# Moving GpSimd's rounding and scaling of the last attention head to other engines, and reordering four hand-overs of a mixture-of-experts layer

## What is computed

```
x = x + attention(layernorm(x))     # 12 heads of 32, scores + row bias + column bias, softmax, @ w_proj + b_proj
t = layernorm(x)                    # 8 groups of 128 tokens
probs = softmax(t @ w_router); gate, idx = top_k(probs, 2)
slot of a token in its expert = running count within the group, first choices ahead of second; at most C = 40
expert_in[e] = dispatch^T @ t       # (8 groups * 40 slots) x 384
out = combine @ (relu(expert_in[e] @ wi[e]) @ wo[e])     # wi 384 x 1536, wo 1536 x 384, 8 experts
x = x + out
```

## Time and profile before

| | |
|---|---|
| median of 3 executions | 580.09 us (579.93 to 580.94) |
| the profiled execution | 579.37 us, its span 577.6 us |
| TensorE, matmuls | busy 561.6 us, 97% |
| VectorE | 389.5 us, 67% |
| ScalarE | 281.2 us, 49% |
| GpSimd | 192.5 us, 33% |
| granted clock of TensorE, mean | 0.998 |
| a matmul of the experts, 128x320 | 309 to 311 ns |
| ScalarE rounding 128x1152 (`woh`) | 1167 ns |
| GpSimd comparing 128x640 (`dsp`) | 1.83 us |

### The profile page before, as it was taken

How to read it: one execution, slowest core, us unless ns; L and a number is a source line. 1 busy time by engine, 2 the same in 40 slices (tenths; PEclk the granted TensorE clock), 3 DMA queues, 4 the chain that set the end, 5 groups by cost and what they waited for, 6 DMA issues and landing times.

```text
span 577.6 us, 11988 instructions
## 1 busy us (share of the span) xinstructions
PE 561.6 (97%) x4673; PEld 466.2 (81%) x4673; DVE 389.5 (67%) x817; ACT 281.2 (49%) x397; POOL 192.5 (33%) x130
## 2 busy tenths in 40 slices
PE   8999999999999999999899999999999999999996
PEld 7787765555555555559879999999999999999994
DVE  6647887888888888257999844554675455467524
ACT  4454234555555555544564354444454444545424
POOL 2200027888888888996430000000000000000002
PEclk9999999999999999999999999999999999999999
DMA  7356047555555550130606255443533444344203
GB/s 224 91 109 134 15 105 149 110 112 107 108 109 110 102 112 17 42 111 5 202 11 235 84 164 165 138 152 122 165 113 133 165 153 148 111 164 137 70 1 110
DMA packets 42917, 66.61 MB, mean 115 GB/s; under 512 B 5058, under 2 KB 35640, under 8 KB 42742
## 3 DMA queue, kind: packets, MB, share of 16 engines
q1 hardware_dynamic: 42870, 65.98, 41.8%
HBM read 44.42 MB, written 1.57 MB: 80 GB/s over the span
## 4 chain that ended last, share of the span: by engine, by line
PE 84%; POOL 5%; DVE 4%; ACT 4%; issue 2%; POOLq 0%; ACTq 0%; DVEq 0%
PE ps L940 22%; PE ps L956 22%; PE ps L716 10%; PE ps L708 9%; PE ps L601 8%; PE ps L689 5%; POOL acc L509 3%; ACT prob L1122 2%; PE ps L967 1%; PE ps L566 1%; PE ps L634 1%; POOL acc L503 1%; DVE tl L1467 1%; PE ps L645 1%; POOL dsp L540 1%
## 5 line engine op out<-in xcount | busy, mean ns | idle before, releaser
L1122 ACT ACTIVATE prob<-ps 128x1024 f32<-128x1024 f32 x96 | 94.5, 1023 | 92.9 <-PE ps L708 91.1
L509 POOL TENSOR_TENSOR acc<-acc,prob 128x1024 f32<-128x1024 f32 x47 | 113.0, 2404 | 5.5 <-POOL acc L509 0.5
L940 PE MATMUL ps<-xeh,wih 128*128 128x320 f32 x288 | 89.6, 311 | 1.0 <-ACT xeh L1179 1.0
L956 PE MATMUL ps<-hh,woh 128*128 128x320 f32 x288 | 89.2, 310 | 0.0
L956 PE MATMUL ps<-hh,wol 128*128 128x320 f32 x288 | 89.0, 309 | 0.0
L940 PE MATMUL ps<-xeh,wil 128*128 128x320 f32 x288 | 89.0, 309 | 0.0
L956 PE MATMUL ps<-hl,woh 128*128 128x320 f32 x288 | 89.0, 309 | 0.0
L940 PE MATMUL ps<-xel,wih 128*128 128x320 f32 x288 | 89.0, 309 | 0.0
L548 POOL CAST dpc<-dpt 120x1024 fp32r<-120x1024 f32 (+1 forms) x3 | 3.1, 1041 | 240.6 <-PE ps L976 216.5
L708 PE MATMUL ps<-qm,km 64*128 64x512 f32 x576 | 79.3, 398 | 1.7 <-ACT prob L1122 0.6
L1460 DVE TENSOR_TENSOR wol<-raw_o,woh 128x1152 fp32r<-128x1152 f32 x32 | 43.4, 1357 | 50.8 <-ACT woh L1154 50.8
(11 more groups left out here) (172 smaller groups left out, 943.9 us busy)
## 6 DMA issues: line engine op xcount, KB each, us to landing
raw_i<-in_L_ffn_wi SPq DMA_DIRECT2D x32, 576.0 KB, 5.2
raw_o<-in_L_ffn_wo SPq DMA_DIRECT2D x32, 576.0 KB, 4.2
km<-kp SPq DMA_DIRECT2D x24, 256.0 KB, 4.0
qm<-qh SPq DMA_DIRECT2D x24, 192.0 KB, 4.0
xs<-in_x SPq DMA_DIRECT2D x8, 384.0 KB, 4.7
qm<-relw SPq DMA_DIRECT2D x24, 128.0 KB, 4.0
qm<-relh SPq DMA_DIRECT2D x48, 64.0 KB, 2.3
qm<-ql SPq DMA_DIRECT2D x24, 64.0 KB, 2.9
```

The source lines that it names most:

```text
L509: nc.gpsimd.tensor_tensor(acc[:, :], acc[:, :], prob[:, slot_of(j, t), :], ALU.add).then_inc(sum_add, 1)
L940: last = mm(bank(k, SLOTS), w[:, b, c, k * P:(k + 1) * P], xe[:, c, e, :], start=c == 0 and n == 0, stop=c == DC - 1 and n == 2)
L956: last = mm(bank(3 + c, SLOTS), w[:, b, k, c * P:(c + 1) * P], h[:, b, k, :], start=s == 0 and k == 0 and n == 0, stop=s == UNITS - 1 and ...
L1122: run(prob[:, slot_of(j, t), :], ps[:, 2 * (t % 2) * BANK:2 * (t % 2 + 1) * BANK], ACT.Exp).then_inc(exp_done, 1)
```

## The change

Four places are touched.

- Last head: GpSimd no longer rounds `wph` (ScalarE does, after head 10's exponentials) nor scales head 10 (VectorE does, with the reciprocal in bank 7). `wpl` on VectorE waits until GpSimd's last addition is done. SP loads `wpj` ahead of the row of maxima of head 11.
- Routing: `number0` comes ahead of `low(1)`, and the low part of the first expert weights goes to GpSimd, behind `tl`.
- First unit: the first bank of hidden(0) waits for eleven of twelve copies ahead of its first chunk, for none ahead of the second and for the twelfth ahead of the third.
- Last combine: the last unit's output is computed chunk by chunk, each chunk with a signal of its own (`y_last`). The turn three groups on comes ahead of a sum. Group 6 is added by VectorE, and ScalarE issues the last store.

```diff
--- before.py
+++ after.py
@@ -220,6 +220,7 @@
             sem(n) for n in ("h_mm", "h_hi", "h_lo", "y_mm", "eo_ready", "eo_last", "c_left", "c_pooled"))
+        y_last = sem("y_last")
         round_set, c_turned, c_hi, c_lo, c_mm, c_added, out_done = (
@@ -295,7 +296,7 @@
         TURN_BANKS, SUM_BANKS, AHEAD = [6, 0, 1, 2], [7, 3, 4, 5], 3
-        WHOLE, POOLED = (0, 3, 7), (1, 4, 6)
+        WHOLE, POOLED = (0, 3, 7), (1, 4)
@@ -429,11 +430,11 @@
                     gather_head(h + 2)
-                if h + 1 < NH:
-                    max_row(h + 1)
                 if h == NH - 2:
...
                     sp.dma_start(wpj[:, :, :], w_proj.rearrange("(c p) n -> p c n", p=P)).then_inc(wpj_in, 16)
+                if h + 1 < NH:
+                    max_row(h + 1)
@@ -454,7 +455,7 @@
-            for t in range(NT):
+            for t in range(NT - 1):
                 sp.wait_ge(*added(t))
@@ -496,12 +497,12 @@
-            def add_probs(h, j, added=ADDED):
+            def add_probs(h, j, added=ADDED, scale=True):
...
                 nc.gpsimd.tensor_tensor(acc[:, :], prob[:, slot_of(j, 0), :], prob[:, slot_of(j, 1), :], ALU.add).then_inc(sum_add, 1)
-                if not isinstance(h, int) or h > 0:
+                if scale and (not isinstance(h, int) or h > 0):
                     normalise(h - 1)
@@ -516,9 +517,7 @@
             add_probs(NH - 2, (NH - 2) % 3)
-            pool.wait_ge(wpj_in, 16)
-            nc.gpsimd.tensor_copy(wph[:, :, :], wpj[:, :, :]).then_inc(wp_hi, 1)
-            add_probs(NH - 1, (NH - 1) % 3, LAST_ADDED)
+            add_probs(NH - 1, (NH - 1) % 3, LAST_ADDED, scale=False)
@@ -531,6 +530,10 @@
                 nc.gpsimd.tensor_copy(th[:, t, :], tn[:, t, :]).then_inc(th_ready, 1)
+
+            pool.wait_ge(wi_hi, 1)
+            pool.wait_ge(tl_ready, NT)
+            nc.gpsimd.tensor_tensor(wil[:, 0, :, :], raw_i[:, 0, :, :], wih[:, 0, :, :].bitcast(F32), ALU.subtract).then_inc(wi_lo, 1)
@@ -911,9 +914,6 @@
                     last.then_inc(xe_mm, 1)
-            pe.wait_ge(xe_act, STEPS)
-            pe.wait_ge(xe_dve, STEPS)
-
             def slot_side(n):
@@ -936,6 +936,9 @@
                     for c in range(DC):
+                        if v == 0 and k == 0 and c != 1:
+                            pe.wait_ge(xe_act, STEPS - (c == 0))
+                            pe.wait_ge(xe_dve, STEPS - (c == 0))
                         for n, (w, xe) in enumerate(terms):
@@ -949,13 +952,25 @@
                     wait(pe, eo_ready, DC * e)
+
+                def chunk(k, c):
+                    for n, (w, h) in enumerate([(woh, hh), (woh, hl), (wol, hh)]):
+                        last = mm(bank(3 + c, SLOTS), w[:, b, k, c * P:(c + 1) * P], h[:, b, k, :],
+                                  start=s == 0 and k == 0 and n == 0,
+                                  stop=s == UNITS - 1 and k == UF - 1 and n == 2)
+                    return last
+
+                if v == E * UNITS - 1:
+                    pe.wait_ge(h_lo, UF * E * UNITS)
+                    for c in range(DC):
+                        for k in range(UF):
+                            last = chunk(k, c)
+                        last.then_inc(y_last, 1)
+                    return
                 for k in range(UF):
...
                     for c in range(DC):
-                        for n, (w, h) in enumerate([(woh, hh), (woh, hl), (wol, hh)]):
-                            last = mm(bank(3 + c, SLOTS), w[:, b, k, c * P:(c + 1) * P], h[:, b, k, :],
-                                      start=s == 0 and k == 0 and n == 0,
-                                      stop=s == UNITS - 1 and k == UF - 1 and n == 2)
+                        last = chunk(k, c)
                     if k == UF - 1:
@@ -1024,6 +1039,11 @@
             for g in range(NT):
+                if g + AHEAD < NT:
+                    if g + AHEAD >= 4:
+                        former = g + AHEAD - 4
+                        pe.wait_ge(*((c_hi, NT * (NR - 1) + former + 1) if former in WHOLE else (c_lo, lows(former))))
+                    combine_turn(NR - 1, g + AHEAD, TURN_BANKS[(g + AHEAD) % 4])
                 if g >= 4:
@@ -1033,11 +1053,6 @@
                     combine_sum(NR - 1, g, SUM_BANKS[g % 4], lows(g))
-                if g + AHEAD < NT:
-                    if g + AHEAD >= 4:
-                        before = g + AHEAD - 4
-                        pe.wait_ge(*((c_hi, NT * (NR - 1) + before + 1) if before in WHOLE else (c_lo, lows(before))))
-                    combine_turn(NR - 1, g + AHEAD, TURN_BANKS[(g + AHEAD) % 4])
@@ -1133,6 +1148,8 @@
             exps(NH - 2, (NH - 2) % 3, lambda t: None)
+            act.wait_ge(wpj_in, 16)
+            run(wph[:, :, :], wpj[:, :, :], ACT.Copy).then_inc(wp_hi, 1)
@@ -1182,11 +1199,11 @@
-            def leave(r, k, chunks=range(DC)):
+            def leave(r, k):
...
                 wait(act, c_turned, NT * r)
-                for c in chunks:
+                for c in range(DC):
                     run(eoT[:, c, :, k, :], bank(3 + c, SLOTS).rearrange("p (g s) -> p g s", s=C), ACT.Copy).then_inc(eo_ready, 1)
@@ -1233,12 +1250,16 @@
                 experts(r)
-            leave(NR - 1, 1, [0, 2])
+            wait(act, c_turned, NT * (NR - 1))
+            for c in (0, 2):
+                act.wait_ge(y_last, c + 1)
+                run(eoT[:, c, :, 1, :], bank(3 + c, SLOTS).rearrange("p (g s) -> p g s", s=C), ACT.Copy).then_inc(eo_ready, 1)
             for g in range(NT):
...
                     leave_sum(g - 2)
-            leave_sum(POOLED[-1])
+            act.wait_ge(*added(NT - 1))
+            act.dma_start(out_v[:, NT - 1, :], xs[:, NT - 1, :]).then_inc(out_done, 16)
@@ -1363,7 +1384,7 @@
-            def normalise(h):
+            def normalise(h, k=6):
@@ -1371,10 +1392,10 @@
                 parts = osb[:, :].rearrange("p (s b d) -> p s b d", s=2, b=NT)
-                ve.reciprocal(bank(6, NT), parts[:, 1, :, 0]).then_inc(o_rec, 1)
+                ve.reciprocal(bank(k, NT), parts[:, 1, :, 0]).then_inc(o_rec, 1)
                 dve.wait_ge(o_rec, h + 1)
                 ve.tensor_tensor(attn[:, h // HPG, :, h % HPG * HD:(h % HPG + 1) * HD], parts[:, 0, :, :],
-                                 bank(6, NT).unsqueeze(2).broadcast_to([P, NT, HD]), ALU.mult).then_inc(o_normed, 1)
+                                 bank(k, NT).unsqueeze(2).broadcast_to([P, NT, HD]), ALU.mult).then_inc(o_normed, 1)
@@ -1433,9 +1454,10 @@
             attn_low(0)
-            turn_output(NH - 2)
+            normalise(NH - 2, 7)
             attn_low(1)
             dve.wait_ge(wp_hi, 1)
+            dve.wait_ge(sum_add, (ADDED - 1) * (NH - 1) + LAST_ADDED - 1)
             ve.tensor_tensor(wpl[:, :, :], wpj[:, :, :], wph[:, :, :].bitcast(F32), ALU.subtract).then_inc(wp_lo, 1)
@@ -1472,8 +1494,6 @@
             ve.tensor_copy(tnT[:, 1, BANK:2 * BANK], bank(4)).then_inc(turn_dve, 1)
-            low(1)
-            split_wi(0, 0)
@@ -1489,6 +1509,7 @@
             step(ve.tensor_scalar(number0[:, :], slot1[:, 0:E], -1.0, None, ALU.add))
+            low(1)
             dve.wait_ge(logits_mm, 1)
@@ -1587,13 +1608,15 @@
+            dve.wait_ge(wi_lo, 1)
             split_wi(1, 1)
...
                 experts(r)
-            dve.wait_ge(y_mm, UNITS * E)
+            dve.wait_ge(c_turned, NT * (NR - 1))
+            dve.wait_ge(y_last, 2)
             ve.tensor_copy(eoT[:, 1, :, 1, :], bank(4, SLOTS).rearrange("p (g s) -> p g s", s=C)).then_inc(eo_last, 1)
...
```

## The result

The changed kernel takes 577.59 us (median of 6, 577.35 to 577.83) against 580.01 us for the kernel before beside it (6 runs, 579.9 to 581.72). The ratio is 0.9946, 95% interval 0.9932 to 0.996: faster, clear of the noise though by less than half a per cent, some 2.4 us by the medians. The forecast was 577.3 (576.1 to 579.1).

What follows compares the result with a forecast made beforehand. TensorE carries 84% of the chain, so only stretches where the chain leaves it can shorten: 0.55 + 0.62 + 0.51 + 1.08 = 2.76 us off, from the median of 580.09 to 577.3 us, range 576.1 to 579.1.

Steps and rivals of the forecast that it cites:

- Last head: Head 11's sum to the projections: sum ends 1.40 earlier, `wpl` follows it, projections start earlier; 0.55 us gained.
- Routing: Low part of first expert weights moved to GpSimd: logits' maximum starts 0.62 us earlier, then limited by TensorE's logits.
- First unit: First expert unit: TensorE starts 0.75 earlier on eleven copies, but the second unit waits for `hl`; 0.51 us left.
- Last combine: Last unit's output by chunk (0.34), tile 7's store issued earlier by ScalarE, landing in 1.9; 1.08 us together.
- the 0.90 counted for the sum: Last head: with `wpl` waiting for the sum, GpSimd's last addition takes 2.40 instead of 3.30; 0.90 us gained.
- The front rival (5th): Sum irrelevant as `wpl` ends at 257.2 anyway, first unit awaits another copy: 0.55 and 0.51 lost, 578.4; 6%.
- the lower bound of 2.7: Routing: least time priced for GpSimd's subtraction, scaled from its additions; 2.8 us taken, upper bound 3.3.
- A sign that the prediction named as one of being wrong: Last combine: a pause inside the sums would show the forecast wrong; no size given.
- the first: Rival, last head: x arrives before the sum is done, a bias addition precedes `wpl`; 1.6 us lost, 578.9; 10%.
- the second rival: Last combine: the store on ScalarE's queue lands like SP's first load, 1.2 us later, 578.5; 13%.
- the third: Rival, routing: the port holds VectorE until 283.4; up to 2.35 us lost, 579.7; 7%.
- the fourth: Rival, slower: `wpl` held behind a bias addition, logits' maximum behind the subtraction; 581.3, or 581.8 with a 3.3 subtraction; 4%.

Runs made afterwards that it cites:

- wpl_no_wait: The changed kernel with `wpl` not waiting for GpSimd's sum; 578.28 us, ratio 0.9957 to the kernel before.
- turns_undone: The changed kernel with the turn behind the sum again in the last combine; 577.65 us, ratio 0.996 to the kernel before.
- store_sp: The changed kernel with SP issuing all eight stores, the last behind tile 6's; 578.29 us, ratio 0.9962 to the kernel before.
- wil_twice: The changed kernel with GpSimd making the low part of the first expert weights twice, same result; 580.25 us, ratio 0.9996 to the kernel before.
- wpl_gap: The changed kernel with `wpl` in the gap where GpSimd waits between heads 10 and 11; 577.7 us, ratio 0.9951 to the kernel before.
- tail_order: The changed kernel with only VectorE's order of low parts and adds in the last combine changed; 578.39 us, ratio 0.9954 to the kernel before.
- all_new: The changed kernel with the `wpl_gap` and `tail_order` edits, plus the first unit's first-bank `hl` ahead of gates and `wol`; 577.73 us, ratio 0.9945.

## Why the prediction was right

The forecast was 577.3, the measured time 577.59. By stretches it was 2.36 us instead of 2.76; three of the four terms came within 0.1, partly against each other (0.06 and 0.05 too much, 0.09 too little), and one was clearly too large.

**Last head**, forecast 0.55, measured 0.49 between the kernels and 0.50 undone. The sum's end was forecast 1.40 earlier and came 1.43 earlier (19.50 against 20.93); `wpl` took 1.36. The reasoning "the sum no longer decides, `wpl` does" is what `wpl_no_wait` shows, and its other side: the 0.90 counted for the sum buys nothing. The front rival (5th) had right that the sum no longer decides, and was wrong that the 0.55 would fall away with it: `wpl` ended at 256.6 on the axis of the kernel before, not at 257.2.

**Routing**, forecast 0.62, measured 0.71 and 0.68 undone. The start was given a hand-over of 0.10 behind the logits; it was 0.04. `number0` cost 0.30 instead of 0.16 beside GpSimd's casts, and was hidden. GpSimd's subtraction took 2.63, under the lower bound of 2.7.

**First unit**, forecast 0.51, measured 0.46: 0.70 less the pause of 0.24.

**Last combine**, forecast 1.08, measured 0.70 (0.86 - 0.53, plus 3.18 - 2.78, less 0.03 in the stretch between). This is the term that was mis-sized: the step that failed is taking 1.9 for the landing, the row for a store that was not slowed by others. The issue of the last store came 1.03 earlier, nearly as forecast, and 0.04 after the addition. Its landing took 2.34, 0.33 more than that of the last store before (2.01), because it was the fourth of a row that lands 0.52 to 0.56 apart. The forecast walked tile 7 and its store and never asked when tiles 4, 5 and 6 would land. This term makes up all of the error of the sum but 0.02: 2.76 forecast, 2.36 measured by stretches, 2.42 by the medians.

A sign that the prediction named as one of being wrong did appear: a pause of 0.40 inside the sums. It cost nothing, as `turns_undone` shows, so the sign was badly chosen. The pause ahead of the first turn was 0.53, forecast 0.45.

**The rivals.** x came 0.3 after `wpl` had begun, so the first was near. ScalarE's store took 0.3 longer to land than SP's last one before, a quarter of what the second rival had; but `store_sp` shows that it isn't the queue. `wil_twice` settles the third and the fourth: the maximum of the logits, MAX8 and the index searches are not held, and both cases needed that they were. The shares that the prediction adds for its range (0.60, 0.13, 0.06 and half of 0.10) give 0.84, not 0.82; nothing hangs on it.

## What to carry to other kernels

When two waits end close together, price an edit by the distance to the second one: 1.35 us taken off VectorE were worth 0.68, an earlier start of 0.70 was worth 0.46, and 0.9 saved on GpSimd's sum was worth nothing because the work moved behind it took its place. Beside GpSimd, place VectorE's instructions with two SBUF inputs in its gaps, as in `wpl_gap`, and look at their durations, since a held instruction shows no idle time. When a kernel ends in several stores issued close together, count back from the first of the row: here the last landed 0.52 to 0.56 behind each one before it, whoever issued it. Compare kernels that differ by half a microsecond stretch by stretch from a common instruction; the medians here could not tell these parts apart.

## What was not expected

**The granted clock near the start moves everything behind it.** `mneg` of head 11 lies between 235.66 and 238.24 in these profiles, for the same work ahead of it. The stretches 8 to 12, 12 to 16 and 16 to 20 us of two kernels whose start is the same code follow. Behind the length come the busy times and counts of TensorE's matmuls, its weight loads, VectorE, ScalarE and GpSimd; the last three columns are the granted clock, the DMA engines' share and GB/s. First the changed kernel:

```profile
8.00:12.00 4.00, 3.03 (x24) 2.42 (x22) 3.40 (x13) 2.59 (x7) 1.80 (x3) 1.00 0.89 267
12.00:16.00 4.00, 2.31 (x16) 2.00 (x17) 3.60 (x7) 2.63 (x5) 2.00 (x5) 1.00 0.54 135
16.00:20.00 4.00, 4.00 (x19) 3.31 (x18) 3.20 (x9) 1.74 (x3) 0.00 (x0) 1.00 0.61 207
```

Then `wpl_no_wait`:

```profile
8.00:12.00 4.00, 2.81 (x22) 2.37 (x21) 3.50 (x13) 2.74 (x6) 0.83 (x2) 1.00 0.88 257
12.00:16.00 4.00, 1.83 (x12) 1.48 (x12) 3.60 (x7) 2.39 (x4) 2.98 (x6) 0.90 0.33 104
16.00:20.00 4.00, 3.86 (x13) 3.13 (x13) 3.48 (x10) 0.90 (x2) 0.00 (x0) 0.68 0.87 268
```

There TensorE's first turn came at 9.17 instead of 8.78, since the second of the x loads landed at 5.42 instead of 5.03 (the first turn comes 3.75 after that landing in these profiles); TensorE was then busy 1.83 of the 4 us from 12 to 16 instead of 2.31, and the granted clock fell to 0.90 and then 0.68 of full (a mean of the two levels, 2.4 and 1.2 GHz, over the stretch). `mneg` came 2.24 later. In `wil_twice`, `tail_order` and `all_new` the clock in these stretches fell to between 0.50 and 0.87, and `mneg` came at 237.4 to 237.7. In the ten other profiles the clock was full there and `mneg` came before 236.4. What lets the clock fall is open: `turns_undone` had its first turn as late, at 9.25, and kept the full clock. It was not tried with a run of its own. The late turn itself costs little: `mneg` of `turns_undone` came 0.29 after that of the changed kernel.

**Two edits against the same queue.** Tile 6 on VectorE and the last store on ScalarE brought 0.40 together; undone singly they cost 0.13 and 0.01, since behind both the row of four stores stands as the next limit.
